# A recommendation tower on one core: more split pairs, and low parts dealt between VectorE and GpSimd

## The reference

```python
e = stack([tbl_f[ids[:, f]] for f in range(39)], axis=1)          # b, field, d
for W, bias in ((w0, b0), (w1, b1), (w2, b2)):                    # w0: 39x39x128, w1, w2: 39x64x128
    z = relu(einsum('bhd,bkd,hks->bsd', e, xk, W) + bias)
    xk, direct = z[:, :64], z[:, 64:]                             # the last layer keeps all 128 as direct
logit = sum(concat(directs), axis=-1)                             # over d
h = relu(relu([logit, dense_ctx] @ W_top1 + b) @ W_top2 + b) @ W_top3
```

## Time and profile before

| | us |
|---|---|
| Median of 3 runs | 677.37 (675.78 to 678.53) |
| Profiled execution, first to last instruction | 674.9 |
| PE busy | 638.7 (95%) |
| DVE busy | 588.5 (87%) |
| POOL busy | 314.3 |
| ACT busy | 253.3 |

### The profile page before, as it was taken

The page is one execution under the profiler, slowest core; times in us unless marked ns, Lnnn a source line. Parts: engine busy times, 40 slices in busy tenths (PEclk is TensorE's granted clock), DMA queues, the critical chain, the costliest instruction groups (busy, mean ns, idle before and its releaser), DMA issues.

```text
span 674.9 us, 6021 instructions
## 1 busy us (share of the span) xinstructions
PE 638.7 (95%) x1878; PEld 350.3 (52%) x1878; DVE 588.5 (87%) x550; ACT 253.3 (38%) x331; POOL 314.3 (47%) x392
## 2 busy tenths in 40 slices
PE   0777899999999999999999999999999999999998
PEld 0334455555555555555555555555555555555554
DVE  0258598999999999999999999999999999999950
ACT  1122324444444344343344443443433434433322
POOL 6775655436455453546364454536364132122320
PEclk9999699999999999999999999999999999999999
DMA  9689826985757759393857568583948476090200
GB/s 199 171 257 347 236 97 200 286 323 140 259 181 217 246 151 311 73 336 85 317 139 251 194 180 282 149 304 68 341 94 289 155 230 221 13 298 1 68 0 2
DMA packets 126751, 130.12 MB, mean 193 GB/s; under 512 B 60734, under 2 KB 68686, under 8 KB 126719
## 3 DMA queue, kind: packets, MB, share of 16 engines
q1 hardware_dynamic: 117743, 128.23, 59.0%
q0 software_dynamic: 5120, 1.32, 2.1%
q10 hardware_dynamic: 3856, 0.18, 0.4%
HBM read 123.31 MB, written 6.39 MB: 192 GB/s over the span
## 4 chain that ended last, share of the span: by engine, by line
PE 86%; POOL 2%; issue 2%; DMA 2%; DVE 1%; ACT 0%; DVEq 0%; ACTq 0%; POOLq 0%
PE z L677 55%; PE z L667 9%; PE z L668 8%; PE z L669 8%; DMA bc<-fields 2%; POOL emb L333 2%; PE z L684 1%; PE z L685 1%; PE z L750 1%; DVE low L585 1%; PE top L740 1%; DVE raw L601 0%; PE tp L740 0%; PE z L740 0%; PE xk L756 0%
## 5 line engine op out<-in xcount | busy, mean ns | idle before, releaser
L677 PE MATMUL z<-whole,w 128*128 128x512 f32 (+2 forms) x928 | 428.8, 595 | 1.7 <-DVE whole L609 1.0
L677 PEld LDWEIGHTS z<-whole,w 128*128 128x128 f32 (+2 forms) x928 | 175.4, 190 | 157.9 <-issue 140.4
L609 DVE TENSOR_TENSOR whole<-bc,xk 128x1024 f32<-128x1024 f32 (+1 forms) x208 | 231.5, 1134 | 21.5 <-PE z L677 11.6
L436 ACT ACTIVATE high<-raw 128x1024 fp32r<-128x1024 f32 (+1 forms) x128 | 135.4, 1059 | 295.4 <-DVE raw L601 239.0
L333 POOL DMA_INDIRECT emb<-in_tables,rows_all x160 | 168.2, 1052 | 57.4 <-issue 52.4
L585 DVE TENSOR_TENSOR low<-raw,high 128x1024 fp32r<-128x1024 f32 (+1 forms) x128 | 161.5, 1262 | 9.1 <-ACT high L436 9.1
L667 PE MATMUL z<-high,w_high 128*128 128x512 f32 (+1 forms) x256 | 143.7, 561 | 6.6 <-DVE low L585 4.6
L601 DVE TENSOR_TENSOR raw<-bc,xk 128x1024 f32<-128x1024 f32 x112 | 136.0, 1214 | 0.0
L351 POOL TENSOR_TENSOR stack<-stack_raw,stack 64x512 fp32r<-64x512 f32 x32 | 43.6, 1362 | 190.1 <-ACT stack L443 184.0
L668 PE MATMUL z<-high,w_low 128*128 128x512 f32 (+1 forms) x256 | 101.7, 397 | 0.0
L669 PE MATMUL z<-low,w_high 128*128 128x512 f32 (+1 forms) x256 | 101.4, 396 | 0.0
(11 more groups left out here) (61 smaller groups left out, 198.9 us busy)
## 6 DMA issues: line engine op xcount, KB each, us to landing
bc<-fields SPq DMA_DIRECT2D x64, 1024.0 KB, 6.8
rot<-fields SPq DMA_DIRECT2D x16, 1280.0 KB
bc<-fields SPq DMA_DIRECT2D x16, 768.0 KB
rot<-fields SPq DMA_DIRECT2D x16, 512.0 KB
fields<-xt SPq DMA_DIRECT2D x64, 80.0 KB
bc<-fields SPq DMA_DIRECT2D x32, 128.0 KB
rep<-fields SPq DMA_DIRECT2D x48, 80.0 KB
emb<-in_tables,rows_all POOLq DMA_INDIRECT x160
```

Of the source, the lines that this page charges most:

```text
L436: act.activation(high[0:m, k % PART_SLOTS], raw[0:m, k % RAW_SLOTS], ACT.Copy).then_inc(high_ready, 1)
L609: nc.vector.tensor_tensor(whole[0:rows, n % WHOLE_SLOTS, 0:len(tiles)], left, right, ALU.mult).then_inc(whole_ready, 1)
L677: ins = nc.tensor.matmul(z[layer][:, :], w[layer][0:m, WHOLE_AT[layer, t], :], whole[0:m, k % WHOLE_SLOTS, u], start=(t == 0), stop=(layer ...
```

## The change

Thirteen pairs a phase are split where there were eight. A table of kinds says for each pair of a layer whether it is whole (w), split with its low part on VectorE (v), or split with its low part on GpSimd (g); v0 below is pair 0 of a layer, of kind v. `TAKEN` is the order in which PE takes a layer's pairs.

```diff
-SPLIT = {0: (1,), 1: (2, 4, 6, 8), 2: (2, 5, 8)}
+KIND = {0: "vwww", 1: "vwgvgwvgww", 2: "vgwvwggvww"}
+TAKEN = {0: (1, 0, 2, 3), 1: (1, 0, 2, 3, 5, 4, 6, 8, 7, 9), 2: (2, 0, 1, 4, 3, 8, 5, 9, 6, 7)}
-PART_SLOTS = 4
+PART_SLOTS = {"v": 2, "g": 2}
+HALF_TILE_AT = 8
```

```diff
-                if g in SPLIT[layer]:
-                    k = SPLIT_NO[layer, c, g]
+                if KIND[layer][g] == "v":
+                    k = NO["v"][layer, c, g]
+                    if k:
+                        dve.wait_ge(low_ready["v"], k)
+                    else:
+                        dve.wait_ge(dense_ready, 1)
+                    nc.vector.tensor_tensor(raw_bank[0:m], left, right, ALU.mult).then_inc(raw_ready["v"], 1)
+                    pending.append([-1, (layer, c, g)])
+                elif KIND[layer][g] == "g":
+                    k = NO["g"][layer, c, g]
                     if k >= RAW_SLOTS:
-                        dve.wait_ge(low_ready, k + 1 - RAW_SLOTS)
-                    nc.vector.tensor_tensor(raw[0:m, k % RAW_SLOTS], left, right, ALU.mult).then_inc(raw_ready, 1)
-                    pending.append([-1, (layer, c, g)])
+                        dve.wait_ge(low_ready["g"], k + 1 - RAW_SLOTS)
+                    nc.vector.tensor_tensor(raw[0:m, k % RAW_SLOTS], left, right, ALU.mult).then_inc(raw_ready["g"], 1)
```

On ACT, `layer2_out(p - 1)` and the high part of layer 0 change places at the start of a phase:

```diff
             for p in range(1, CHUNKS + 1):
-                if p + 2 in IN:
-                    for g in SPLIT[0]:
-                        high_part(0, p + 2, g)
...
                 layer2_out(p - 1)
+                if p + 2 in IN:
+                    high_parts(0, p + 2)
                 if p + 1 in IN:
-                    high_part(1, p + 1, SPLIT[1][0])
+                    high_parts(1, p + 1, 0, 3)
                 if p + 3 in IN:
                     turned(p + 3)
```

```diff
+                if more:
+                    gather(p + 4, range(0, 2))
+                fold2(p - 1)
+                if third:
+                    low_part(1, p + 1, 0)
+                if more:
+                    gather(p + 4, range(2, 5))
+                if third:
+                    low_part(1, p + 1, 1)
+                    low_part(1, p + 1, 2)
                     stack_part(1, p + 1)
...
+                if third:
+                    fold01(p + 1)
+                if second:
+                    stack_part(2, p)
```

More of the change, by code:

```diff
@@ L176, in tower @@
         d_ready = [sem(f"d_ready{n}") for n in range(3)]
-        d_free = [sem(f"d_free{n}") for n in range(3)]
+        d_free01 = sem("d_free01")
+        d_free2 = sem("d_free2")
         folded = sem("folded")
@@ L354, in fold @@
[L354 to L364, removed]
+                pool.tensor_tensor(stack[0:KEEP, :], stack_raw[0:KEEP, :], stack[0:KEEP, :], ALU.subtract).then_inc(stack_low, 1)
@@ new lines, in low_part, with sums @@
+            def low_part(layer, c, i):
+                k, m = NO["g"][layer, c, groups_of(layer, "g")[i]], ROWS[layer]
+                pool.wait_ge(high_ready["g"], k + 1)
+                pool.tensor_tensor(low["g"][0:m, k % PART_SLOTS["g"]], raw[0:m, k % RAW_SLOTS], high["g"][0:m, k % PART_SLOTS["g"]], ALU.subtract).then_inc(low_ready["g"], 1)
+            def sums(n, src, column, c, read, read_to):
+                width = N // 2
+                pool.tensor_tensor(halves[0][:, :], src[:, 0:width], src[:, width:2 * width], ALU.add).then_inc(read, 1)
+                pool.wait_ge(read, read_to)
+                pool.tensor_tensor(halves[1][:, :], halves[0][:, 0:width // 2], halves[0][:, width // 2:width], ALU.add).then_inc(folded, 1)
@@ L369, in fold @@
-                issued["folds"] += 1
-            for c in range(4):
-                gather(c)
-            landed(2)
-            landed(3)
-            fold(0, 0)
-            stack_part(1, 0)
[L377 to L381, removed]
-            stack_part(2, 0)
-            own_done()
-            gather(5)
-            landed(5)
+                pool.tensor_tensor(logits[:, column, c * SUB:(c + 1) * SUB], halves[2][:, 0:SUB], halves[2][:, SUB:2 * SUB], ALU.add).then_inc(folded, 1)
@@ new lines, in fold01, with fold2 @@
+            def fold01(c):
+                pool.wait_ge(d_ready[0], c + 1)
+                pool.wait_ge(d_ready[1], c + 1)
+                sums(FOLDS * FOLD_NO["01", c], direct01[c % 2], 0, c, d_free01, c + 1)
+            def fold2(c):
+                pool.wait_ge(d_ready[2], c + 1)
+                sums(FOLDS * FOLD_NO["2", c], direct2, 1, c, d_free2, c + 1)
+            for c in range(3):
+                gather(c)
+            low_part(1, 0, 0)
+            gather(3, range(0, 2))
+            low_part(1, 0, 1)
@@ L386, in _ @@
+            gather(3, range(2, 4))
+            low_part(1, 0, 2)
+            stack_part(1, 0)
+            gather(3, range(4, 6))
+            low_part(2, 0, 0)
+            gather(3, range(6, GATHERS))
+            low_part(2, 0, 1)
+            low_part(2, 0, 2)
+            fold01(0)
+            stack_part(2, 0)
+            gather(4, range(0, 3))
+            low_part(1, 1, 0)
+            gather(4, range(3, 6))
+            low_part(1, 1, 1)
+            low_part(1, 1, 2)
             stack_part(1, 1)
-            fold(0, 2)
@@ L388, in _ @@
-            fold(1, 1)
+            gather(4, range(6, GATHERS))
+            fold01(1)
             for p in range(1, CHUNKS + 1):
[L390 to L395, removed]
-                    stack_part(1, p + 1)
-                if p + 2 in IN:
[L398 to L401, removed]
+                more, third, second = p + 4 in IN, p + 1 in IN, p in IN
+                if more:
[8 more added lines that the diff above has]
+                    low_part(1, p + 1, 2)
+                    stack_part(1, p + 1)
+                if more:
+                    gather(p + 4, range(5, 6))
+                if second:
+                    low_part(2, p, 0)
+                if more:
+                    gather(p + 4, range(6, 8))
+                if second:
+                    low_part(2, p, 1)
+                    low_part(2, p, 2)
+                if more:
+                    gather(p + 4, range(8, GATHERS))
+                if third:
+                    fold01(p + 1)
+                if second:
@@ L429, in left_factor, with high_parts @@
                 act.activation(left0, rep[:, :], ACT.Copy).then_inc(left_ready, 1)
[L431 to L436, removed]
+            def high_parts(layer, c, first=0, end=GATHERS):
+                for g in groups_of(layer, "vg")[first:end]:
+                    kind = KIND[layer][g]
+                    k, m, slots = NO[kind][layer, c, g], ROWS[layer], PART_SLOTS[kind]
+                    src = raw_bank[0:m] if kind == "v" else raw[0:m, k % RAW_SLOTS]
+                    act.wait_ge(raw_ready[kind], k + 1)
+                    if k >= slots:
+                        act.wait_ge(parts_free[kind], k + 1 - slots)
+                    act.activation(high[kind][0:m, k % slots], src, ACT.Copy).then_inc(high_ready[kind], 1)
             def stack_part(layer, c):
```

228 lines of the change are left out of this document (115 added, 113 removed).

## The result

The changed kernel takes 704.39 us (703.67 to 704.6) against 676.58 for the kernel before (the median of four runs now). The medians divide to 1.041; the ratio given with the result is 1.043 (95% interval 1.0388 to 1.0472): 4% slower. Its profiled execution has a span of 702.3.

A forecast was written before the change was run, and what follows sets the result against it. TensorE bound the kernel before at 37.36 us a phase; a loop of waits was to bind at 39.5. Eleven phases +23.5, two +3.3, end +4, start -4: +26.8 on 674.9, 701.7, so 704 us, range 687 to 724.

The forecast's parts named there:

- The ring: Loop from layer 2's last stack on TensorE through ScalarE, VectorE's first low part and TensorE back: 38.8 us a phase.
- the bound for v products right behind a low part: On VectorE, three v products waiting for the low part just ahead lose overlap: 0 to 0.3 us a phase.
- POOL's loop: Second loop, through GpSimd's low parts, gathers and stacks: 37.9 to 39.8 us a phase; 39.5 taken as the longer.
- The price of PSUM: VectorE's v products and low parts using PSUM: no difference taken, bound -1.2 to +1.2 us a phase.
- no change: Rival: PSUM makes 12 VectorE instructions 0.12 us shorter each, loop 37.4, start and end cancel: 677 us, chance 0.06.
- PE's saving: On TensorE, ten more split tiles a phase, each 0.16 us cheaper: 1.6 us less, 35.8 left.
- The upper end of 3.43 for POOL's low part: GpSimd's 128x1024 low part: 2.35 us taken, 3.43 if 1.08 us is added as in a sum that started with VectorE's low part.
- The sum: Whole span: 26.8 us added to 674.9 gives 701.7; the median lies 2.5 us above, so 704.
- The last two: Last two phases, which have the same stall: about 2 us each, +4 in all.
- The start: Start of the kernel, where most of TensorE's 4.96 us wait for the first stack goes: -4 us, bounds 0 and -10.
- POOL as the bound: Rival: GpSimd is the bound outright, 40.6 us a phase, 716 us, chance 0.25.
- PE stays the bound, 649 us: Rival: TensorE still bounds and the change is faster by 28 us, if layer 0's low part needn't wait; chance 0.05.

The follow-up runs named there:

- experiment 1: Changed kernel with ScalarE's high parts of layer 0 put back ahead of layer 2's output: 654.22 us, ratio 0.9663; again 653.82 us, 0.9694.
- experiment 2: Kernel before, with only layer 2's output on ScalarE put ahead of the high part of layer 0: 697.04 us, ratio 1.0295.
- experiment 3: Changed kernel with GpSimd's low parts made for a pair's first tile only, part of the computation left out: 705.65 us, ratio 1.0429.
- experiment 4: Changed kernel with the v products in an SBUF buffer in place of PSUM: 788.78 us, ratio 1.1663.
- experiment 7: Changed kernel with high parts ahead of layer 2's output, also in the last two phases, and GpSimd's low part there ahead of its sum: 648.53 us, 0.9605.
- experiment 5: Changed kernel with v products in SBUF and GpSimd's low parts made for the first tile only, part of the computation left out: 709.51 us, ratio 1.0525.

## Why the prediction was right

The time came out at 704.39 for 704, the span at 702.3 for 701.7. The mechanism is the one forecast, and experiments 1 and 2 show it from both sides. That the sum fits to 0.6 us is partly luck: it has errors of both signs.

- **The ring.** Forecast 1.70 + 28.45 + 1.27 + 7.38 = 38.8. Measured from the rows of the loop, with low0 of the phase at 277.56: 316.80 - 315.13 = 1.67; 306.42 - 277.56 = 28.86; 307.68 - 306.42 = 1.26; 315.13 - 307.68 = 7.45. Marks that follow each other around a period always add up to it, 39.24 here. What makes these the ring is that nobody on them waits in between: DVE has no gap over 0.10 us from low0 to w8, and PE none from w8 to T. The 0.41 on DVE is the bound for v products right behind a low part, put at 0 to 0.3 and left out of the 38.8. DVE's timeline from that low part on shows such a pair:

```profile
277.56 1.23 DVE L609 TENSOR_TENSOR low_v<-raw_bank,high_v 120x1024 fp32r<-120x1024 f32 x1 [3.91 <-ACT high_v L468]
...
282.69 1.21 DVE L609 TENSOR_TENSOR low_v<-raw_bank,high_v 128x1024 fp32r<-128x1024 f32 x1
283.94 1.23 DVE L627 TENSOR_TENSOR raw_bank<-bc,xk 128x1024 f32<-128x1024 f32 x1
```

  A step of 1.25, not 1.1325, and 1.25 and 1.31 for the other two: 0.41 more in all.
- **POOL's loop: the step that was wrong.** "As the longer of two coupled loops I take 39.5" did not hold. Behind a stack or a low part the first gather comes after about 0.15 us, where 0.30 and 0.76 were the two ends (the 0.76 of the earlier trace rows stands behind a stack, not behind a sum, and the terms with it add up to 39.7, not 39.8); POOL waits no more for its own results there. POOL's timeline around the stack that closes a phase, and its first low part:

```profile
312.54 0.25 POOL L369 TENSOR_TENSOR logits<-sum 128x32 f32<-128x32 f32 x1
312.75 1.29 POOL L352 TENSOR_TENSOR stack<-stack_raw,stack 64x512 fp32r<-64x512 f32 x1
...
314.19 0.96 POOL L347 DMA_INDIRECT emb<-in_tables,ids_all  x1 [0.15 <-issue]
...
323.17 2.39 POOL L358 TENSOR_TENSOR low_g<-raw,high_g 128x1024 fp32r<-128x1024 f32 x1 [4.76 <-ACT high_g L468]
```

  The stack is ready at 314.04, PE takes it at 314.51, without a wait. The period is the same 39.24 without gathers, where 39.0 was forecast, and experiment 3 settles it: half the work, no gain.
- **Sizes on DVE and POOL.** POOL's low part was put at 2.35 and has a mean of 2.39. The price of PSUM was put at nothing: low parts from it take 1217 ns, from SBUF 1216 to 1269 before; so the rival "no change", which needed 0.12 us less of each, falls too. PE's saving was put at 1.6 us a phase, 35.8 left; where PE is full, in experiment 1, its phase is 35.36. By the Trainium skill, page "VectorE: DVE Perf Modes", section "The TRN2 errata — SBUF-src ops pay a fixed extra latency per instruction", 65 ns more were due (an estimate from that page); the rows here don't show them. The upper end of 3.43 for POOL's low part needed the holds of a low part read from SBUF; experiment 4 shows them, and that PSUM removes them. That is the rule of the Trainium skill, "SBUF — State Buffer", section "Who interferes with whom": a DVE instruction with two inputs in SBUF and a GpSimd one that reads SBUF shut each other out, one with a single SBUF input doesn't. The rows of experiment 4 show its first half and those of the changed kernel its second. The prediction had no row for the second half, but the trace of before has one: POOL's sum of 0.46 at 320.08 ran beside a DVE product with one input in PSUM (320.04, 1.22 us), both at full pace.
- **The sum.** Thirteen phases were to add 26.8; phase 1 adds 2.7 and the twelve others 22.5, 25.2 in all. The last two were to add 4, and add 2.2 each. The start was to give 4 and gave 2.2 (the stack that opens phase 1 starts at 116.52, was 118.73). The first stack waits no more and the clock of 60:100 is 0.96 where it was 0.87, but PE comes to the stack hardly earlier, having waited elsewhere, first 6.17 us for DVE's dense parts (1.67 before); PE's timeline of the start:

```profile
26.63 11.45 PE L735 MATMUL z<-w,ident 128*128 128x512 f32 x22 [6.17 <-DVE dense_parts L602]
...
53.05 2.80 PE L722 MATMUL z<-whole,w 128*128 128x512 f32 x4 [2.08 <-DVE whole L640]
...
69.47 0.79 PE L729 MATMUL z<-stack,w_high 128*128 128x512 f32 x1
```

  The first stack starts at 69.47 instead of 69.69. Which of the edits at the start brought these waits wasn't tried.
- **The rivals.** POOL as the bound falls by experiment 3. "PE stays the bound, 649 us" was the changed kernel without the order on ACT, and experiments 1 and 7 measured it: 654 and 648.5. It named the right condition, low0 not waiting for T.

## What to carry to other kernels

Where an engine runs a fixed program, an instruction that waits for the end of one phase must not stand ahead of one that another engine needs to start the next: busy shares of 81 and 89% with nobody full were the sign here, and the chain of idle rows (PE waits for DVE, DVE for ACT, ACT for PE) names the place. Count the ring from one such wait to the next; where its sum exceeds every engine's own, as 38.8 did 35.8 here, expect it as the period. After breaking one, look for the next instruction that waits for the same event: here it was on POOL.

## What had not been expected of the hardware

How much such a hold can cost. In experiment 4 a DVE low part with both inputs in SBUF and POOL's low parts, stacks and sums ran one after the other, and the one that waits can wait for several in a row: DVE's low part of 1.21 us took 6.12 behind two low parts and a stack of POOL's. Where the two programs keep meeting, in the phases with gathers, the period went from 39.23 to 46.0, and the kernel lost 84 us (788.78 against 704.39, different runs). In the two phases without gathers, and with POOL's low parts half as long, DVE's holds were short, 1.80 and 1.46 us its longest low parts, and a phase took 39.5 in both; the ratio of experiment 5 is 1.0525, beside 1.0429 in experiment 3. Gathers, which POOL starts, were held as well, 0.81 to 0.84 us beyond the end of DVE's low part.
